# The third layer norm of a block is not stored: the unnormalized sum is scaled per token in the addition behind the down projection

## What is computed

```python
def _layernorm(x, axis=-1, eps=1e-05):
    m = jnp.mean(x, axis=axis, keepdims=True)
    v = jnp.var(x, axis=axis, keepdims=True)
    return (x - m) / jnp.sqrt(v + eps)
...
def _L1_ffn_ref(x, ln_gamma, ln_beta, fc1_q, ...):
    residual = x
    h = (x - mu) * jax.lax.rsqrt(var + EPS) * ln_gamma + ln_beta
    y = jax.nn.silu(hf @ w1 + fc1_bias)
    z = y @ w2 + fc2_bias
    return residual + 0.5 * z.reshape(residual.shape)
...
x = _layernorm(x + _L1_attn_ref(x, ...), axis=-1)
x = _layernorm(x + _L1_ffn_ref(x, ...), axis=-1)
```

## Time and profile before

| | us |
|---|---|
| three runs | 1088.25, 1092.7, 1092.55; median 1092.55 |
| the profiled execution | 1091.53 |
| its span | 1089.7 |
| mean granted clock of PE, as a share of full | 0.966 |
| busy in the span: PE, DVE, ACT, POOL | 977.5, 934.5, 847.9, 716.1 |

### The profile page before, as it was taken

How to read it: one execution, slowest core, us unless ns; L and a number is a source line. 1 busy time by engine, 2 the same in 40 slices (tenths; PEclk the granted TensorE clock), 3 DMA queues, 4 the chain that set the end, 5 groups by cost and what they waited for, 6 DMA issues and landing times. The chain is left out here.

```text
span 1089.7 us, 17921 instructions
## 1 busy us (share of the span) xinstructions
PE 977.5 (90%) x5598; PEld 738.8 (68%) x5598; DVE 934.5 (86%) x1232; ACT 847.9 (78%) x1650; POOL 716.1 (66%) x603
## 2 busy tenths in 40 slices
PE   6999999999978999998657599999999989997987
PEld 4677777777754555555545487777777777786776
DVE  7999999999963897965799999999999999999851
ACT  7778878878746668767877889898998989897843
POOL 3456466766761111323779999998989989998630
PEclk9999999999998999999778799999999999999899
DMA  6443434433415002112987768477676757776401
GB/s 187 124 143 114 139 110 141 122 94 116 120 52 195 0 1 78 39 39 88 245 167 168 137 155 170 118 179 153 164 147 164 151 135 188 151 151 141 88 4 38
DMA packets 93921, 133.86 MB, mean 123 GB/s; under 512 B 8706, under 2 KB 48642, under 8 KB 93828
## 3 DMA queue, kind: packets, MB, share of 16 engines
q1 hardware_dynamic: 93828, 132.73, 49.1%
HBM read 116.45 MB, written 14.16 MB: 120 GB/s over the span
## 5 line engine op out<-in xcount | busy, mean ns | idle before, releaser
L2345 DVE TENSOR_TENSOR_SCAN oa<-bank_a,h,oa 128x512 f32<-128x512 f32 x128 | 159.7, 1269 | 12.7 <-ACT h L2020 9.8
L2345 DVE TENSOR_TENSOR_SCAN ob<-bank_a,h,ob 128x512 f32<-128x512 f32 x128 | 160.1, 1268 | 10.2 <-ACT bank_a L2011 6.1
L1820 PE MATMUL bank_m<-w,f_h 128*128 128x256 f32 x448 | 104.3, 383 | 0.0
L1491 POOL TENSOR_TENSOR oa<-ob,x1T 128x1024 f32<-128x1024 f32 x8 | 18.8, 2355 | 129.5 <-DVE ob L1391 129.5
L2011 ACT ACTIVATE bank_a<-s,A 128x512 f32<-128x512 f32 x128 | 86.8, 684 | 17.8 <-DVE ob L2345 8.9
L2011 ACT ACTIVATE bank_a<-dtc,A 128x512 f32<-128x512 f32 x128 | 86.9, 684 | 14.1 <-DVE ob L2345 6.9
L1765 PE MATMUL bank_y<-ident,ob 128*128 128x128 f32 x512 | 71.2, 285 | 26.1 <-POOL ob L2581 14.4
L1820 PEld LDWEIGHTS bank_m<-w,f_h 128*128 128x128 f32 x448 | 84.7, 192 | 14.2 <-issue 3.6
L1765 PEld LDWEIGHTS bank_y<-ident,ob 128*128 128x128 f32 x512 | 62.6, 147 | 36.6 <-POOL ob L2581 15.3
L883 POOL TENSOR_TENSOR xd<-xs,L 128x512 f32<-128x512 f32 x32 | 34.0, 1063 | 76.1 <-DVE xs L662 76.1
L1765 PE MATMUL bank_y<-ident,oa 128*128 128x128 f32 x512 | 70.9, 284 | 14.1 <-DVE oa L2351 14.0
(11 more groups left out here) (403 smaller groups left out, 2925.8 us busy)
## 6 DMA issues: line engine op xcount, KB each, us to landing
Bb<-CB_rows SPq DMA_DIRECT2D x128, 256.0 KB, 6.1
Cb<-CB_rows SPq DMA_DIRECT2D x128, 256.0 KB, 5.8
abc<-decays SPq DMA_DIRECT2D x32, 512.0 KB, 4.4
Ebc<-ramps SPq DMA_DIRECT2D x64, 128.0 KB, 3.1
uT<-in_uT SPq DMA_DIRECT2D x8, 512.0 KB, 4.2
u<-in_u SPq DMA_DIRECT2D x8, 512.0 KB, 3.9
x_tokens<-x2s SPq DMA_DIRECT2D x8, 512.0 KB, 3.5
x_rows<-x1T SPq DMA_DIRECT2D x8, 512.0 KB, 2.9
```

Source lines behind the costliest of these rows:

```text
L1820: i = e.matmul(to, f_h[:, k, c * CH:(c + 1) * CH], w2[:, k, :], start=False, stop=(c % 2 == 1 and k == KF - 1))
L2345: e.tensor_tensor_scan(s[:, k, :], p_a[k][:, :], s[:, k, :], h0[:, n, k:k + 1], ALU.mult, ALU.add).then_inc(v_s, 1)
```

## The change

norm4's output is not written any more. `second` reads the unnormalized sum in `xl` itself, multiplies it per token by `twice4`, which is 2 * rs4, and adds the down projection; the shift by the mean falls away, because norm6 takes the mean out again. `twice4` comes out of the same power instruction with the constants changed by a factor of four (0.25/DM and 0.25 EPS ahead of it, 4 EPS in norm5's scale). A factor per token is a factor per partition and chunk, so `second` needs one instruction per chunk instead of one for two chunks. `xl` has to live until `second`, a round longer, so there are two of it (`xl[b % 2]`), and two of `twice4`; `x3` is gone. The waits for `a_x3` are gone; `norm45` waits for `second` of the block two before, ahead of writing `twice4`. The end functions are changed in the same way; the last block's sum is formed in place in `xl`.

```diff
-            xl, xn, x3, x3b = (t(n, [P, NC, DM])[:, :, :] for n in ("xl", "xn", "x3", "x3b"))
+            xl, (xn, x3b) = many("xl", [P, NC, DM]), (t(n, [P, NC, DM])[:, :, :] for n in ("xn", "x3b"))
...
+            twice4 = many("twice4", [P, NC])
...
-                def norm4(b, p):
-                    e.wait_ge(p_l4, 9 * b + 9)
-                    after(e, v_x3b, 2 * b)
-                    for c in (2 * p, 2 * p + 1):
-                        e.activation(x3[:, c, :], xl[:, c, :], ACT.Identity, bias=nb4[:, c:c + 1], scale=rs4[:, c:c + 1]).then_inc(a_x3, 1)
...
-                    if 0 <= last < NB - 1:
-                        norm4(last, 0)
...
-                    if 0 <= last < NB - 1:
-                        norm4(last, 1)
...
-                end_norm4(0)
...
-                end_norm4(1)
...
                 def residual(b, p):
                     if p == 0:
                         e.wait_ge(ld_x2, DMAS * (b + 1))
-                        after(e, a_x3, 4 * b)
...
                 def second(b, p):
                     e.wait_ge(pe_dn, 2 * b + p + 1)
-                    e.wait_ge(a_x3, 4 * b + 4)
                     after(e, st_o, DMAS * b)
-                    e.scalar_tensor_tensor(x3b[:, 2 * p:2 * p + 2, :].rearrange("p c f -> p (c f)"), x3[:, 2 * p:2 * p + 2, :].rearrange("p c f -> p (c f)"),
-                                           2.0, pair[p][:, :], ALU.mult, ALU.add).then_inc(v_x3b, 1)
+                    for c in (2 * p, 2 * p + 1):
+                        i = e.scalar_tensor_tensor(x3b[:, c, :], xl[b % 2][:, c, :], twice4[b % 2][:, c:c + 1],
+                                                   pair[p][:, (c % 2) * DM:(c % 2 + 1) * DM], ALU.mult, ALU.add)
+                    i.then_inc(v_x3b, 1)
...
                 def norm45(b):
                     e.wait_ge(v_l4, 2 * b + 2)
                     e.sem_inc(step, 1)
-                    e.tensor_scalar(ve4[:, :], mv4[:, :, 1], 1.0 / DM, EPS, ALU.mult, ALU.add).then_inc(p_l4, 1)
+                    e.tensor_scalar(ve4[:, :], mv4[:, :, 1], 0.25 / DM, 0.25 * EPS, ALU.mult, ALU.add).then_inc(p_l4, 1)
                     e.wait_ge(p_l4, 9 * b + 1)
-                    e.sem_inc(step, 1)
-                    e.tensor_tensor(rs4[:, :], ve4[:, :], mhalf[:, 0:NC], ALU.pow).then_inc(p_l4, 1)
+                    after(e, v_x3b, 2 * b - 2)
+                    e.sem_inc(step, 1)
+                    e.tensor_tensor(twice4[b % 2][:, :], ve4[:, :], mhalf[:, 0:NC], ALU.pow).then_inc(p_l4, 1)
...
                 def end_second(p):
                     if p == 0:
                         e.wait_ge(a_n6, 4 * Z)
                     e.wait_ge(pe_dn, 2 * Z + p + 1)
-                    e.wait_ge(a_x3, 4 * Z + 2 * p + 2)
-                    e.scalar_tensor_tensor(halves(x3)[p], halves(x3)[p], 2.0, pair[p][:, :], ALU.mult, ALU.add).then_inc(v_x3b, 1)
+                    for c in (2 * p, 2 * p + 1):
+                        i = e.scalar_tensor_tensor(xl[Z % 2][:, c, :], xl[Z % 2][:, c, :], twice4[Z % 2][:, c:c + 1],
+                                                   pair[p][:, (c % 2) * DM:(c % 2 + 1) * DM], ALU.mult, ALU.add)
+                    i.then_inc(v_x3b, 1)
```

More of the change, by code:

```diff
@@ L1559, in build @@
             pe_y, pe_D, pe_gt, pe_o, pe_ft, pe_up, pe_dn = (d_sem("pe_" + n) for n in ("y", "D", "gt", "o", "ft", "up", "dn"))
-            a_a, a_c, a_hs, a_zs, a_gt, a_n3, a_xn, a_x3, a_ft, a_up, a_fs, a_n6 = (d_sem("a_" + n) for n in (
-                "a", "c", "hs", "zs", "gt", "n3", "xn", "x3", "ft", "up", "fs", "n6"))
+            a_a, a_c, a_hs, a_zs, a_gt, a_n3, a_xn, a_ft, a_up, a_fs, a_n6 = (d_sem("a_" + n) for n in (
+                "a", "c", "hs", "zs", "gt", "n3", "xn", "ft", "up", "fs", "n6"))
             v_s, v_g, v_gate, v_pre, v_l3, v_l4, v_l6, v_x3b = (d_sem("v_" + n) for n in ("s", "g", "gate", "pre", "l3", "l4", "l6", "x3b"))
@@ L1636, in end_store @@
                     e.wait_ge(a_n6, 4 * Z + 2 * p + 2)
-                    e.dma_start(out.rearrange("(n p) f -> p n f", p=P)[:, Z * NC + 2 * p:Z * NC + 2 * p + 2, :], x3[:, half[p], :]).then_inc(st_o, DMAS)
+                    e.dma_start(out.rearrange("(n p) f -> p n f", p=P)[:, Z * NC + 2 * p:Z * NC + 2 * p + 2, :], xl[Z % 2][:, half[p], :]).then_inc(st_o, DMAS)
                 def early_loads(e):
@@ L2121, in end_normed @@
                     e.activation(nT_h[:, :, p * DM:(p + 1) * DM], wide[p][:, :].rearrange("p (k t) -> p k t", k=KD), ACT.Copy).then_inc(a_ft, 1)
-                def end_norm4(p):
-                    if p == 0:
-                        e.wait_ge(v_x3b, 2 * Y + 2)
-                    e.wait_ge(v_b, 4 + 2 * p)
-                    for c in (2 * p, 2 * p + 1):
-                        e.activation(x3[:, c, :], xl[:, c, :], ACT.Identity, bias=nb4[:, c:c + 1], scale=rs4[:, c:c + 1]).then_inc(a_x3, 1)
                 def end_hidden(p, m):
@@ L2403, in end_residual @@
                         e.wait_ge(ld_x2, DMAS * NB)
-                        e.wait_ge(a_x3, 4 * Z)
                     e.wait_ge(pe_o, 2 * Z + p + 1)
-                    e.tensor_tensor(halves(xl)[p], wide[p][:, :], halves(x2)[p], ALU.add).then_inc(v_pre, 1)
+                    e.tensor_tensor(halves(xl[Z % 2])[p], wide[p][:, :], halves(x2)[p], ALU.add).then_inc(v_pre, 1)
                     e.wait_ge(v_pre, 2 * Z + p + 1)
-                    e.bn_stats(both_of(st3, p), turnwise(xl, p)).then_inc(v_l3, 1)
+                    e.bn_stats(both_of(st3, p), turnwise(xl[Z % 2], p)).then_inc(v_l3, 1)
                     e.wait_ge(v_l3, 2 * Z + p + 1)
@@ L2438, in end_scales @@
                     e.sem_inc(step, 1)
-                    e.tensor_scalar(sq4[:, h], sq4[:, h], 1.0 / DM, EPS, ALU.mult, ALU.add).then_inc(v_e, 1)
+                    e.tensor_scalar(sq4[:, h], sq4[:, h], 1.0 / DM, 4.0 * EPS, ALU.mult, ALU.add).then_inc(v_e, 1)
                     e.wait_ge(p_l4, 9 * Z + 2 * p + 2)
-                    e.tensor_tensor(rs5[:, h], rs4[:, h], ve4[:, h], ALU.mult)
+                    e.tensor_tensor(rs5[:, h], twice4[Z % 2][:, h], ve4[:, h], ALU.mult)
                     e.wait_ge(v_b, 3 + 2 * p)
@@ L2634, in norm45 @@
                     e.sem_inc(step, 1)
-                    e.tensor_tensor(rs5[:, :], rs4[:, :], sq4[:, :], ALU.mult)
+                    e.tensor_tensor(rs5[:, :], twice4[b % 2][:, :], sq4[:, :], ALU.mult)
                     e.tensor_tensor(nb5[:, :], nb4[:, :], sq4[:, :], ALU.mult).then_inc(p_l4, 1)
@@ L2646, in summed @@
                     e.sem_inc(step, 1)
-                    e.tensor_tensor(xl, xl, x2, ALU.add).then_inc(p_add, 1)
+                    e.tensor_tensor(xl[b % 2][:, :, :], xl[b % 2][:, :, :], x2, ALU.add).then_inc(p_add, 1)
                 def drive(b):
@@ L2669, in end_root4 @@
                 def end_root4(p):
-                    end_root(rs4[:, half[p]], ve4[:, half[p]], 3 + 2 * p, p_l4)
+                    end_root(twice4[Z % 2][:, half[p]], ve4[:, half[p]], 3 + 2 * p, p_l4)
                 def end_root5(p):
```

40 lines of the change are left out of this document (20 added, 20 removed).

## The result

The changed kernel takes 1096.03 us (median of 20 runs, 1092.2 to 1099.5) and the kernel before, run beside it, 1091.69 us (median of 19). The ratio is 1.0032, with a 95% interval of 1.0021 to 1.0044: slower by 2.3 to 4.8 us, which is less than the 0.5% that the prediction names. Forecast were 1094.2 us and a range of 1088.0 to 1098.0. The profiled execution took 1093.06 us with a span of 1091.2 us, 1.5 us more than before.

What follows compares the result with a forecast made beforehand. The prediction took the bound to be a loop of DVE, then ACT and PE to the gate, then ACT's burst. Steady blocks 2.1 and tail 0.6 added 2.7 us to 1091.53, giving 1094.2 us, range 1088.0 to 1098.0.

Steps and rivals of the forecast that it cites:

- What bounds the kernel: Last layer's blocks, period 64.3 us: DVE from 872 to about 893, ACT and PE to the gate, the burst, DVE again.
- the block from 615: Block 615 to 679, without `second`: 2.5 us less DVE work yet just as long, explained by DVE waiting 1.63 us.
- Part 1: Norm4 leaving ACT, 13.7 us of its time over 7 blocks: gains 0, because ACT waits for DVE scans anyway.
- Part 2: DVE's `second` in four pieces of 0.40 against 1.18 us: +0.42 us per block, 2.1 us over five blocks.
- The bound without the factor: `second` on DVE, if reading the factor cost nothing: four pieces of 0.32 make 1.28 us, +0.10 per block.
- rival A: Slower: `second`'s small pieces do not overlap what follows, +0.86 per block, +6.5 us in all, 1098.0 us; chance 0.12.
- The sixth `second`: At 1005 us, last steady block: its delay is absorbed by DVE's later 2.46 us wait for PE at the gate, 0.
- Part 3: Tail: three pieces of `second` on the chain that ended last go from 0.60 to 0.80 us each, +0.6 us.
- Part 4: Waits for `a_x3` gone, POOL's new wait for `v_x3b` in norm45 always fulfilled, second `xl` buffer removes no wait: 0.
- The sum: 2.1 + 0.6 = +2.7 us on the profiled execution's 1091.53 us: 1094.2 us, chance 0.58.
- B: No cost or little gain: factor's read hidden (+0.10 per block), gate's 0.23 wait gone, -0.8 us, 1090.7 us; chance 0.17.
- C: Faster: ACT is the later engine, so dropping norm4 gains 6.9 to 13.7 us, 1087.3 or 1080.5 us; chance 0.13.

Runs made afterwards that it cites:

- experiment 1: The changed kernel, but `second` is two 512-column instructions with constant factor 2.0; 1091.58 us, ratio 1.0000 to the kernel before.
- experiment 4: The changed kernel with norm4's four instructions back on ACT, written to a tile nobody reads; 1093.48 us, ratio 1.0024 to the kernel before.
- experiment 5: The changed kernel with one more 512-column DVE instruction (SBUF and PSUM operands) ahead of each half of `second`; 1105.10 us, ratio 1.0114 to the kernel before.
- experiment 6: The changed kernel with one more 512-column DVE instruction ahead of each half of `residual`, in the burst; 1094.30 us, ratio 1.0019 to the kernel before.
- experiment 2: The changed kernel, but `second`'s four 256-column instructions use constant factor 2.0; 1093.11 us, ratio 1.0014 to the kernel before.
- experiment 3: The changed kernel, but `second` is two 512-column instructions reading a per-token factor from `twice4`; 1092.73 us, ratio 1.0012 to the kernel before.

## Why the prediction was right

**What bounds the kernel**: right. The loop was read as DVE from `stats4` to about 893, then ACT and PE to the gate, then the burst. ACT's work moves nothing in it (experiments 1 and 4), DVE's moves it one for one ahead of the gate and not at all behind the burst's start up to 1.2 us (5 and 6). One argument for it does not hold as it stands, that the block from 615 is just as long with 2.5 us less DVE work: its 64.26 us stand at a granted clock of 0.92, and at 0.95 the same block took 63.41 to 63.68 (experiments 1 to 4 and 6). The six periods of 64.3 are five of 64.25 and a last one of 63.69.

**Part 1, ACT loses norm4, 0**: right, measured 64.24 against 64.25. The reason given, that ACT waits 0.34 and 0.40 for DVE scans at 893.03 and 906.38, holds in the rows: they are 0.34 and 0.39 after.

**Part 2, +0.42 per block**: right in kind, 0.06 too much. The bound without the factor was +0.10 and came out at 0.13, and the factor, which L709 against L689 priced at 0.08 per piece, costs 0.06. The overlap of 0.08 us at a piece's end is there, since 0.474 us of length stand 0.39 apart. This is also the answer to rival A, which needed 0.51 from start to start. DVE's busy time per block, which the prediction expected about 0.5 us higher, rose by 0.27 (61.65 before, 61.92 after, each from one `stats4` to the next).

**The sixth `second`, 0**: wrong. It was called absorbed by DVE's wait of 2.46 us for PE at the gate. Measured is +0.34 from the last `stats4` to that gate for the change, and +1.21 more with experiment 5, with the wait at 2.53 and 2.55 us. The step that failed is to take a long wait for PE as room. PE's stretch up to the gate begins where ACT hands over f_h, and ACT got there from a decay that had waited for a DVE scan. This is the very loop that the prediction describes for the steady blocks: what is late on DVE ahead of that hand-over makes PE late by as much, and the wait stays as long as it was. ACT's decay and then PE's first instruction behind the hand-over, before (last `stats4` at 1000.18):

```profile
1020.32 0.69 ACT L2011 ACTIVATE bank_a<-s,A 128x512 f32<-128x512 f32 x1
1021.67 0.50 PE L1803 MATMUL bank_m<-nT_h,w_h 128*128 128x512 f32 x1
```

The same two in the change (last `stats4` at 1000.96), then in experiment 5 (1008.46):

```profile
1021.46 0.69 ACT L2012 ACTIVATE bank_a<-s,A 128x512 f32<-128x512 f32 x1 [0.34 <-DVE ob L2327]
1022.81 0.50 PE L1804 MATMUL bank_m<-nT_h,w_h 128*128 128x512 f32 x1 [0.68 <-ACT f_h L2081]
```

```profile
1030.16 0.69 ACT L2013 ACTIVATE bank_a<-s,A 128x512 f32<-128x512 f32 x1 [0.35 <-DVE ob L2328]
1031.51 0.50 PE L1805 MATMUL bank_m<-nT_h,w_h 128*128 128x512 f32 x1 [0.44 <-ACT f_h L2082]
```

Counted from the last `stats4`, the decay starts at 20.14, 20.50 and 21.70, PE at 21.49, 21.85 and 23.05, the gate at 30.98, 31.32 and 32.53: each is late by what DVE was given. PE's clock is no rival for the +0.34, since in this stretch it was lower before (0.89) than in the change (0.95). The parts of the change do not add up here as they do in the steady blocks: from the last `stats4` to the gate experiment 1 has 30.95, experiment 3 31.09, and experiment 2, with the split alone, 31.37, with a wait of 0.19 us for ACT in DVE's list that the change does not have; why is open. The prediction had kept this for rival A ("if the 2.46 wait turns out tied to DVE"); it belonged into the sum, as a sixth block.

**Part 3, the tail, +0.6**: the three distances grew by 0.18, 0.20 and 0.19, which is 0.57. From the gate to the end it is +0.47, as the distances between them came out 0.10 shorter in all, 0.07 of it ahead of the first piece.

**Part 4, waits, 0**: right. Experiment 1 has POOL's new wait and both buffers, and the period of before; and POOL's step behind the new wait begins 0.21 us behind the end of its forerunner, where 0.18 stood before.

**The sum**: +2.7 was predicted for the profiled execution; its traceable part is +2.6 (1.79 + 0.34 + 0.47). That the two are so close is in part luck: of the terms, five blocks came 0.3 below their price, the sixth 0.34 above its 0, and the tail 0.13 below. The 1094.2 is the sum on the profiled execution, and not a value between the two that the prediction names. The medians differ by 4.3 us, and the interval of the ratio, 2.3 to 4.8 us, holds the 2.6 near its lower end. Experiments 4 and 6, with the same distances as the change, gave ratios of 1.0024 and 1.0019, which are 2.6 and 2.1 us. So the surplus of the change's own median over 2.6 has no place in any trace. The eleven runs of the change above 1095 us have a mean granted clock of 0.958 to 0.965, the nine below it 0.963 to 0.969; whether that was chance, or the change makes it likelier, stays open.

**The rivals**: A (1098.0) had the right sign of its extra term for the sixth block only; B (1090.7) asked for the factor's read to be hidden and the gate's 0.23 to go, and both stayed; C (1080.5 to 1087.3) is refuted by experiments 1 and 4.

## What to carry to other kernels

Taking work off an engine is worth what that engine's last wait before the next hand-over lets through; here ACT waited for DVE at both places, so 13.7 us of its work were worth nothing, and the 0.4 us that DVE got in exchange were paid in full. To find whether a wait is room, put known work in front of it and see whether it shrinks: 1.44 us became 0.25, while a wait of 2.5 us for PE did not move, because PE's own start hung on the waiting engine. And a factor that differs per chunk costs twice, once for its read (0.06 us) and once for the split that it forces (0.07 us per cut, start to start).
